# Perceiver kernel on one core: in the first stage, context loads go ahead of X, contexts and table tiles get four buffers each, and X's row statistics stand between the key tiles

## The reference

```python
kv_c   = kv @ w_kv_comp                       # kv: the context, 32 x 256 rows
k_rope = rope(kv_c @ w_k_rope, arange(lk))    # one rotated key row of 64 per context row
qc     = layernorm(x) @ w_q_down              # row mean and variance of x
...
good   = (k_idx <= q_seg) & (k_idx >= q_seg - 2)   # each token looks at up to 3 context rows
scores = where(good, scores, min); attn = softmax(scores)
x = x + (attn @ v) @ w_out
```

## Time and profile before

| | us |
|---|---|
| median of 3 runs (lowest, highest) | 2384.08 (2381.45, 2387.69) |
| the profiled execution | 2398.74 |
| its span | 2397.1 |
| first block, from the span's start to the first TensorE work of the second | 87.7 |

### The profile page before, as it was taken

One profiled execution on the slowest core, in us unless ns is written; L12 is line 12 of the kernel. 1 busy time (PEld: TensorE's weight loads), 2 busy tenths in 40 slices (PEclk: granted clock), 3 DMA queues, 4 the chain that ended last, 5 costly groups with the idle time before them and its releaser, 6 DMA issues. The chain is left out here.

```text
span 2397.1 us, 38628 instructions
## 1 busy us (share of the span) xinstructions
PE 1877.4 (78%) x11288; PEld 1301.8 (54%) x11289; DVE 1560.0 (65%) x3387; ACT 1032.9 (43%) x2950; POOL 1244.9 (52%) x1000
## 2 busy tenths in 40 slices
PE   5599977888897677999979999699547999988000
PEld 5378843333333243677647787587414888776000
DVE  5599938999999968333547777377696333333633
ACT  1376737665656314233247777333215333332000
POOL 1488616766767610688425555366002554543775
PEclk9799988999999977999989999899666999999555
DMA  6311013212212033899601110100503999998342
GB/s 204 106 74 70 11 33 142 78 65 67 75 43 99 0 118 101 197 299 257 149 14 32 32 37 19 29 2 2 189 0 109 285 281 280 276 252 204 111 116 83
DMA packets 163804, 272.04 MB, mean 113 GB/s; under 512 B 28722, under 2 KB 97300, under 8 KB 162708
## 3 DMA queue, kind: packets, MB, share of 16 engines
q1 hardware_dynamic: 130708, 199.72, 25.8%
q0 software_dynamic: 30464, 68.19, 12.4%
q10 hardware_dynamic: 2496, 2.44, 0.4%
HBM read 218.74 MB, written 51.53 MB: 113 GB/s over the span
## 5 line engine op out<-in xcount | busy, mean ns | idle before, releaser
L989 POOL TENSOR_TENSOR b_h<-b_h,b_bcb 128x1024 f32<-128x1024 f32 x128 | 301.9, 2359 | 151.5 <-DVE b_h L1046 150.8
L1558 POOL DMA_INDIRECT m1x_xb<-scratch_xn,m_tok x192 | 182.5, 951 | 336.2 <-DVE m1x_yb L1755 175.9
L814 PE MATMUL b_psy<-b_h,ident 128*128 128x512 f32 x512 | 252.9, 621 | 69.4 <-POOL b_h L989 69.2
L1046 DVE TENSOR_TENSOR_SCAN b_h<-b_dA,b_pbx 128x1024 f32<-128x1024 f32 x128 | 292.6, 2286 | 4.4
L1605 PE MATMUL m1x_psh<-m1x_xe,m1x_w 128*128 128x128 f32 x1536 | 211.4, 281 | 19.9 <-DMA m1x_w<-in_m_w 16.9
L1742 DVE TENSOR_TENSOR m1x_hT<-m1x_sg,m1x_psh 128x128 f32<-128x128 f32 x192 | 55.3, 288 | 235.5 <-ACT m1x_sg L1692 150.7
L814 PEld LDWEIGHTS b_psy<-b_h,ident 128*128 128x128 f32 x512 | 93.6, 193 | 210.4 <-POOL b_h L989 123.1
L945 ACT ACTIVATE b_dA<-b_delta,b_A 128x504 f32<-128x504 f32 x256 | 166.8, 706 | 93.2 <-DVE b_h L1046 87.7
L1605 PEld LDWEIGHTS m1x_psh<-m1x_xe,m1x_w 128*128 128x128 f32 x1536 | 190.4, 195 | 30.0 <-issue 18.1
L1928 POOL TENSOR_TENSOR x_s<-x_s,x_rs 128x1024 f32<-128x1024 f32 x64 | 121.2, 1893 | 126.9 <-DVE x_rs L2094 126.9
L1040 DVE TENSOR_TENSOR b_pbx<-b_pdx,b_bcb 128x1024 f32<-128x1024 f32 x128 | 157.6, 1231 | 19.8 <-ACT b_pdx L928 13.8
(11 more groups left out here) (452 smaller groups left out, 4424.9 us busy)
## 6 DMA issues: line engine op xcount, KB each, us to landing
m1x_w<-in_m_w SPq DMA_DIRECT2D x192, 256.0 KB
b_bcb<-scratch_bc_rows SPq DMA_DIRECT2D x64, 512.0 KB, 4.7
scratch_y<-m1x_yb SPq DMA_DIRECT2D x192, 128.0 KB
m_w<-in_m_w SPq DMA_DIRECT2D x64, 368.0 KB
a_c<-in_ctxT SPq DMA_DIRECT2D x16, 512.0 KB, 3.8
m_w<-in_m_w SPq DMA_DIRECT2D x64, 128.0 KB
x_area<-in_ctxT SPq DMA_DIRECT2D x32, 256.0 KB
m_w2all<-in_m_w SPq DMA_DIRECT2D x1, 8192.0 KB
```

The costliest lines, as they stand in the source:

```text
L814: mm = pe.matmul(psy[:, k % 2, :], ident[:, :], h[:, u % HB, j, :], start=False, stop=(nq == NQ - 1 and j == CQ - 1))
L989: q.tensor_tensor(hs, hs, bcb[:, 1, CQ * nq:CQ * nq + CQ], ALU.mult).then_inc(sem("hc"), 1)
L1046: v.tensor_tensor_scan(h[:, u % HB].rearrange("p j n -> p (j n)"), dA[:, u % DB].rearrange("p j n -> p (j n)"), pbx[:, :, :].rearrange("p ...
L1558: g.indirect_dma_start(out=xb[:, j, :], out_offset=None, in_=xn, in_offset=bass.IndirectOffsetOnAxis(ap=tok[:, b:b + 1], axis=0)).then_inc ...
```

## The change

The first block's five programs are changed; the second block and all later stages are not.

- SP: the contexts of tiles 0 and 1 are issued between the two lists of weights, tiles 2 and 3 after the second. `c` has four buffers (`CR` = 4), so that tile t+4 is loaded into the buffer of tile t.
- ScalarE: the loads of X and `ident` are issued after the copies of the folded weights, which wait for both lists of weights. The square root comes after the store of the mean rows. `tab` has four buffers: the copy of tile t waits for the store of tile t-4.
- VectorE: the indices come first. The loop over the tiles is written out; between `csum` and the rotated half of tile t stands the statistic of X's tile t-3. The rest of the statistics (mean, variance, bias) follow the last tile.
- TensorE and GpSimd: the same work with four semaphores in turn. The PSUM banks stay two.

```diff
-    KR = 4
+    KR, CR = 4, 4
-        c = sb("c", [P, 2, 2, KD, SK])
-        tab = sb("tab", [P, 2, 4, W2])
+        c = sb("c", [P, CR, 2, KD, SK])
+        tab = sb("tab", [P, CR, 4, W2])
...
                     for dst, src in LOADS[n]:
                         sp.dma_start(dst, src).then_inc(sem("weights", n), 16)
-                for u in range(2):
-                    sp.dma_start(c[:, u], ctx_v[u]).then_inc(sem("ctx", u), 16)
-                with sp.Fori(0, NT // 2 - 1) as p:
-                    for u in range(2):
-                        sp.wait_ge(sem("keys_done", u), p + 1)
-                        sp.wait_ge(sem("csum", u), p + 1)
-                        sp.dma_start(c[:, u], ctx_v[2 * p + u + 2]).then_inc(sem("ctx", u), 16)
+                    for r in (0, 1) if n == 0 else range(2, CR):
+                        sp.dma_start(c[:, r], ctx_v[r]).then_inc(sem("ctx", r), 16)
+                with sp.Fori(0, NT // CR - 1) as p:
+                    for r in range(CR):
+                        sp.wait_ge(sem("keys_done", r), p + 1)
+                        sp.wait_ge(sem("csum", r), p + 1)
+                        sp.dma_start(c[:, r], ctx_v[CR * p + r + CR]).then_inc(sem("ctx", r), 16)
...
+                    for r in range(CR):
+                        u, prior = r % 2, (r - 2) % CR
+                        pe.wait_ge(sem("ctx", r), 16 * (p + 1))
+                        pe.wait_ge(sem("rope", prior), p + r // 2)
+                        pe.wait_ge(sem("nope", prior), p + r // 2)
...
             @block.scalar
             def _(a):
-                for n in range(NXL):
-                    lo, hi = n * NT // NXL, (n + 1) * NT // NXL
-                    a.dma_start(X[:, lo:hi, :], d["x"].rearrange("(t p) d -> p t d", p=P)[:, lo:hi, :]).then_inc(sem("x", n), 16)
-                a.dma_start(ident[:, :], d["ident"]).then_inc(sem("ident"), 16)
                 a.wait_ge(sem("wk_prod"), 1)
...
-                ln.scalar_std(a)
...
+                for n in range(NXL):
+                    lo, hi = n * NT // NXL, (n + 1) * NT // NXL
+                    a.dma_start(X[:, lo:hi, :], d["x"].rearrange("(t p) d -> p t d", p=P)[:, lo:hi, :]).then_inc(sem("x", n), 16)
+                a.dma_start(ident[:, :], d["ident"]).then_inc(sem("ident"), 16)
+
+                with a.Fori(0, NT // CR) as p:
+                    for r in range(CR):
+                        a.wait_ge(sem("keys_done", r), p + 1)
+                        a.wait_ge(sem("tab_stored", r), 16 * p)
...
                 a.dma_start(table[KROWS:KROWS + B, :], mrow[:, :]).then_inc(sem("mean_stored"), 16)
+                ln.scalar_std(a)
...
             @block.vector
             def _(v):
-                for n in range(NXL):
-                    v.wait_ge(sem("x", n), 16)
-                ln.vector_tile_stats(v)
-                ln.vector_stats(v)
-                ln.vector_bias(v)
                 v.wait_ge(sem("weights", 1), W_ALL[1])
...
+                LAG = 3
+                for t in range(NT + LAG):
+                    if t < NT:
+                        p, r, u = t // CR, t % CR, t % 2
+                        v.wait_ge(sem("ctx", r), 16 * (p + 1))
+                        v.tensor_reduce(csum[:, :, 2 * t:2 * t + 2].rearrange("p k b -> p b k"), c[:, r], AX_X, ALU.add).then_inc(sem("csum", r), 1)
+                    if t >= LAG:
+                        v.wait_ge(sem("x", (t - LAG) // (NT // NXL)), 16)
+                        ln.vector_one_tile(v, t - LAG)
+                    if t < NT:
+                        v.wait_ge(sem("nope", r), p + 1)
+                        if p:
+                            v.wait_ge(sem("tab_stored", r), 16 * p)
...
+                v.wait_ge(sem("bn"), NT)
+                ln.vector_stats(v)
+                ln.vector_bias(v)
```

More of the change, by code:

```diff
@@ L84, in __init__, with vector_one_tile @@
         self.bias = st.sb("lnbias", [P, NT])
+    def vector_one_tile(self, v, t):
+        v.bn_stats(self.stats[:, t, :], self.e["X"][:, t, :]).then_inc(self.st.sem("bn"), 1)
     def vector_tile_stats(self, v):
-        st, X = self.st, self.e["X"]
         for t in range(NT):
-            v.bn_stats(self.stats[:, t, :], X[:, t, :]).then_inc(st.sem("bn"), 1)
-        v.wait_ge(st.sem("bn"), NT)
+            self.vector_one_tile(v, t)
+        v.wait_ge(self.st.sem("bn"), NT)
     def vector_stats(self, v):
@@ L273, in _ @@
                 pe.wait_ge(sem("wk_copied"), KD)
[L275 to L279, removed]
+                with pe.Fori(0, NT // CR) as p:
+                    for r in range(CR):
[3 more added lines that the diff above has]
+                        pe.wait_ge(sem("nope", prior), p + r // 2)
                         for j in range(4):
                             for k in range(KD):
-                                mm = pe.matmul(psk[:, u, j * P:(j + 1) * P], c[:, u, j // 2, k, (j % 2) * P:(j % 2 + 1) * P],
+                                mm = pe.matmul(psk[:, u, j * P:(j + 1) * P], c[:, r, j // 2, k, (j % 2) * P:(j % 2 + 1) * P],
                                                wk[:, k, :], start=(k == 0), stop=(k == KD - 1))
-                        mm.then_inc(sem("keys_done", u), 1)
-                for u in range(2):
-                    pe.wait_ge(sem("csum", u), NT // 2)
+                        mm.then_inc(sem("keys_done", r), 1)
+                for r in range(CR):
+                    pe.wait_ge(sem("csum", r), NT // CR)
                 for k in range(KD):
@@ L304, in _ @@
                                  ACT.Copy).then_inc(sem("wq_copied"), 1)
-                ln.scalar_std(a)
[L307 to L312, removed]
+                for n in range(NXL):
[3 more added lines that the diff above has]
+                with a.Fori(0, NT // CR) as p:
+                    for r in range(CR):
+                        a.wait_ge(sem("keys_done", r), p + 1)
+                        a.wait_ge(sem("tab_stored", r), 16 * p)
+                        a.activation(tab[:, r, :, 0:KVC], psk[:, r % 2, :].rearrange("p (j c) -> p j c", j=4)[:, :, 0:KVC],
+                                     ACT.Copy).then_inc(sem("nope", r), 1)
                 a.wait_ge(sem("mean_done"), 1)
@@ L322, in _ @@
                 g.memset(clear[:, :], 0.0).then_inc(sem("cleared"), 1)
[L323 to L329, removed]
+                with g.Fori(0, NT // CR) as p:
+                    for r in range(CR):
+                        g.wait_ge(sem("rope", r), p + 1)
+                        g.wait_ge(sem("nope", r), p + 1)
+                        g.dma_start(tab_v[CR * p + r], tab[:, r]).then_inc(sem("tab_stored", r), 16)
+                for r in range(CR):
+                    g.wait_ge(sem("tab_stored", r), 16 * (NT // CR))
             @block.vector
             def _(v):
-                for n in range(NXL):
-                    v.wait_ge(sem("x", n), 16)
-                ln.vector_tile_stats(v)
-                ln.vector_stats(v)
-                ln.vector_bias(v)
                 v.wait_ge(sem("weights", 1), W_ALL[1])
@@ L368, in _ @@
                 v.tensor_copy(idxt[:, :, :].rearrange("p t j -> p j t"), idx[:, :, :]).then_inc(sem("seg"), 1)
[L369 to L374, removed]
-                        kr = psk[:, u, :].rearrange("p (j c) -> p j c", j=4)[:, :, KVC:W2]
[L376 to L379, removed]
-                        v.tensor_tensor(tab[:, u, :, KVC:W2], ra[:, u, 0], ra[:, u, 1], ALU.add).then_inc(sem("rope", u), 1)
```

5 lines of the change are left out of this document (added).

## The result

The changed kernel takes 2359.19 us (median of 4 runs, 2356.36 to 2363.97) against 2383.59 for the kernel before (4 runs). The ratio is 0.9898, with a 95% interval of 0.9876 to 0.9919: 24.4 us less, 19.3 to 29.6 by the interval. Forecast were 2364.8 us, between 2358 and 2374.5, and 19.3 us less.

The account below looks back on a forecast made before the run. Two buffers' circle of `csum`, reload and tile work was taken as the bound. Afterwards DMA: 12.5 + 48.7 / 0.92 = 65.4, last store at 66.4 instead of 85.7; 2384.1 - 19.3 = 2364.8 us, range 2358 to 2374.5.

Parts of the forecast that it names:

- The start: First block up to tile 0: weights landed at 13 us, tile 0 finished at 18.4 instead of 29.1, gaining 10.7.
- the third rival: Start: SP's queue is still held over `cosq`, weights land at 18 to 20 us, saving about 13; chance 0.13.
- VectorE's side of the loop: Tile loop: 2.32 us a tile plus 0.33 per statistic from tile 3 on, tile 15 finished at 57.5 us.
- DMA's side: Loads and stores after 12.5 us: 48.7 us of engine time at a share of 0.92, last store in at 66.4.
- Tile 15: Loop's end: the last tile's copy waits for the store of tile 11, not tile 13; no cost was added.
- The compute side's bound of 60.8: First block's end by compute alone: tile 15 at 57.5, plus 0.64 and 2.7 us for its store.
- the main case: Whole program: the forecast holds, saving 15 to 24 us; chance 0.62.
- the signs that I had named: Profile after: first reload at 18 us, share near 0.92, pace 2.7 to 2.9, no tile 15 store wait, second block near 68.
- Low share: Loop: mixed transfers don't go closer to full, 48.7 us at 0.75 end at 77.4, saving 7 to 12; chance 0.14.
- Starving stores: Loop: stores land late behind a full ring; at 9.0 us landing, 3 us later at the end; chance 0.05.
- the point of 14.7 us: Loop: the store landing time at which the whole gain would be lost, a pace of 4.3 us a tile.
- The tail's statistics: After the last tile: three statistics, mean, variance and bias, 4.1 us, end at 65.1, under the last store's 66.4.

Follow-up runs that it names:

- after_again: The changed kernel itself, profiled and timed a second time: 0.9918 of the kernel before; the second block's TensorE starts at 66.53 us.
- no_wout: The changed kernel without the loads of `vup` and `wout`, both buffers cleared by GpSimd instead; the second block's TensorE starts at 64.77 us.
- c4_tab2: The changed kernel with two table buffers instead of four, still four context buffers: 0.9946 of the kernel before; second block at 76.87 us.
- half_csum: The changed kernel with VectorE's `csum` over one of the two batches of each tile; the second block's TensorE starts at 64.33 us.
- stats_last: The changed kernel with all 16 statistics of X behind the last tile instead of between tiles; the second block's TensorE starts at 65.09 us.
- wout_mid: The changed kernel with `vup` and `wout` issued behind tile 9's context, not the last one: 0.9927 of the kernel before; second block at 72.03 us.
- order_only: The kernel before with the new order of loads and VectorE work, still two buffers of each kind: 0.9974 of its time; second block at 79.59 us.
- split_end: The changed kernel with `wout` loaded in four transfers instead of one, at the same place; the second block's TensorE starts at 65.72 us.
- pieces_mid: The changed kernel with `vup` and four pieces of `wout` issued singly behind the contexts of tiles 11 to 15: 0.9897 of the kernel before; second block at 64.99 us.

## Why the prediction was right

- **The start.** Forecast: weights landed at 13, tile 0 finished at 18.4, 10.7 us earlier. Measured 14.56, 20.23 and 8.9. The last weights were 1.6 us later than the sum of the rings' times, and SP's queue still stood 3.41 us over `cosq`: the third rival's place, at a third of its size. What bound the start in the end was not VectorE, as I had it, but TensorE. I had tile 0's matmuls done by 15.8 and called that enough. `kup` landed at 8.66, not at about 7, the folding took 6.2 us as forecast, and tile 0's 16 matmuls took 3.6 us, not 2.6: 5.12 / 2 is the mean of a slow first tile and a fast second one (from tile 2 on it is 2.02; the granted clock reads 1.00 for both, and why the first is slow isn't shown). So ScalarE's copy was released by TensorE at 18.54, and VectorE stood 0.29 us for it; in after_again, where `kup` landed at 9.73, it stood 1.09.
- **VectorE's side of the loop.** The step was right to the hundredth: 2.32 us a tile without a statistic, 2.65 forecast and 2.64 measured with one. From tile 0 to tile 14 it was 36.3 us; 14 x 2.32 + 12 x 0.33 gives 36.4.
- **DMA's side.** This is the term that was mis-sized. I had priced contexts, X and stores by the packets' time, summed them to 48.7 us of full engines and chosen a share of 0.92, so that the last store was in at 66.4 and DMA was the later of the two sides. With the least landing time, 2.7 us, it was in at 64.4, and from tile 0 to tile 14 VectorE waited for nothing. So the choice of DMA as the later side was wrong: VectorE's list was the bound. The packets' time isn't a fixed price: at a share that reads 1.0 the engines carried 325, 350 and 370 GB/s in three kernels, according to what was asked.
- **Tile 15.** "Copy now waits for the store of tile 11" was in the sum as free. It cost ScalarE 5.6 us and VectorE 1.8 (4.4 and 0.7 in after_again), because the load of `wout` stood in the way. no_wout shows it: tile 15 follows tile 14 by 2.64 us there, by 4.52 in the changed kernel. The compute side's bound of 60.8 became 64.4 by this and the late start.
- **The sum.** 21.3 us were measured for the first block in the profiles against the 19.3 forecast. Two errors of opposite sign met: the start and tile 15 cost 1.8 us each more, DMA 5.6 less (66.4 against 60.8). That 19.3 and 21.3 lie so close is in part luck. The median says 24.4, just above the 15 to 24 of the main case; the 3.1 beyond the first block's lie inside its interval. In the first profile 1.5 us of them are in the second block, where TensorE's clock came back earlier; in after_again that gain isn't there. Of the signs that I had named, SP's reload at 18.92 (for 18) and the second block at 66.38 (for 68) came, while the DMA share (1.02 for 0.92), the pace (2.64 for 2.7 to 2.9) and "no wait of ScalarE for a store at tile 15" did not.
- **The rivals.** Low share: not seen (1.02). Starving stores: the median landing is 4.1 us and the longest 10.0, and up to tile 14 the pace didn't feel them, as the point of 14.7 us said; with two table buffers (c4_tab2) they stopped the loop twice. With a fuller ring beside them the stores' median landing rose from 2.9 to 4.1 us in the first profile, but only to 3.1 in after_again; in half_csum, with 370 GB/s on the engines, it was 6.0. The Trainium skill's rule that each DMA engine goes round its queue rows ("DMA: Bandwidth & Descriptors", section "Queues, rings and completion order") agrees with that direction, which the changed kernel itself hardly shows; it gives no time, and so not the 10.0 us beside one load with long rows. The tail's statistics hid behind the last store as forecast (last instruction at 63.63); stats_last shows the price when they don't.

## What to carry to other kernels

A ring of buffers is a circle: a buffer is loaded, used and freed. Here there were two, loads in and stores out, and deepening one alone gained 2.5 or 2.7 us where both gained 13.2, since the other still stopped the loop: try both before giving up either. Look for single long stops before a mean pace is taken for a period. To see what a loop can reach, take the pace between two iterations that waited for nothing, here 2.32 us, and ask which engine's list that is; it was right to 0.01 us, while a price by the DMA engines' busy share was not. Check which engine the first tile waits for, too: here an earlier `csum` gained nothing, because TensorE's first tile came later. Cut a large weight load with long rows into pieces before it is put beside transfers that something waits for.

## What the runs showed of the hardware

- The DMA busy share isn't a measure of how much room is left. It read 1.02 at 325 GB/s, 1.05 at 350 over 32 us (stats_last), and 1.03 at 370 (half_csum). At 350 GB/s of context reads and table writes, with X in the first part, no tile but the last, behind `wout`, came more than 0.1 us late.
- One load of 1 MB with 16 KB in each of 64 partitions took 9.3 to 11.9 us to land, and contexts of 512 KB behind it 11 us instead of 4 to 5. In four loads with 4 KB rows each landed in 6.8 us (median) and the store beside them in at most 6.8. Why was not measured.
- The clock behind a stall. In wout_mid TensorE stood from 40.4 to 48 us. Its granted clock was 1.00 until 42, 0.61 from 42 to 44 and 0.50 from 44 to 52 (the lower of its two levels, 1.2 GHz), so that tile 10's matmuls took 3.8 us, where a tile at 1.00 took 2.02. Tile 10 comes 7.1 us behind tile 9 instead of 2.64; of these 4.5 us more, 1.8 are the clock's and the rest the wait's. From tile 12 on a tile's matmuls took some 2.0 us again.

```profile
40.00:42.00 2.00, 0.40 (x4) 0.21 (x2) 1.97 (x6) 0.00 (x0) 0.42 (x1) 1.00 0.54 158
42.00:44.00 2.00, 0.00 (x0) 0.00 (x0) 0.38 (x2) 0.00 (x0) 0.33 (x1) 0.61 1.02 371
44.00:46.00 2.00, 0.00 (x0) 0.00 (x0) 0.82 (x4) 0.39 (x1) 0.00 (x0) 0.50 1.05 405
...
50.00:52.00 2.00, 2.00 (x11) 2.00 (x11) 0.00 (x0) 0.17 (x1) 0.00 (x0) 0.50 0.13 50
52.00:54.00 2.00, 2.00 (x17) 2.00 (x16) 1.72 (x5) 0.22 (x1) 0.00 (x0) 0.83 0.48 121
54.00:56.00 2.00, 1.84 (x17) 1.65 (x15) 1.97 (x6) 0.42 (x2) 0.75 (x1) 1.00 0.63 209
```

- The second block begins with TensorE at the lower level in every kernel, but the level rises at very different times. The granted clock was back at 1.00 about 10 us after the block's start in order_only and the first profile of the changed kernel, after 14 to 16 us in eight other profiles, and only after about 26 us in stats_last, no_wout, split_end and pieces_mid. From its beginning to the first addition to X the second block took 55.2 and 55.3 us in the first group, 56.6 to 57.5 in the second (56.7 before, 57.2 in after_again), and 59.2 to 60.7 in the third. No run shows what decides which group a profile falls into. So one profile's time of the second block says nothing of an edit in the first, within some 5 us, and a gain of 1 or 2 us in the first block can be lost behind it.
